# Layer 3 of a four-layer graph network interleaved with the last loop of layer 2's batch norm

## The reference, cut to what matters

```python
x = ...                                     # (128 graphs, 128 nodes, 64 features)
# layer 2: y = (adj @ h + h) @ weight + bias, rows scaled to length 1, then batch norm
cnt  = sum(mask)
mean = sum(y * m, axis=(0, 1)) / cnt
var  = sum((y - mean) ** 2 * m, axis=(0, 1)) / cnt
y    = ((y - mean) / sqrt(var + 1e-5) * gamma + beta) * m
x    = x + relu(y)
# layer 3
h = maximum(layernorm(x), 0)                # over the 64 features of each node
messages = einsum('bij,bjh->bih', adj, h)
dh = tanh(concat([h, messages]) @ W1 + b1) @ W2 + b2
x  = x + dh
```

## Time and profile before

| | us |
|---|---|
| median of 3 runs | 1461.05 |
| lowest and highest | 1458.61, 1461.1 |
| the profiled execution, its own time | 1463.7 |
| its span, first to last instruction | 1462.0 |
| final loop and row scales, 1327.5 to 1376.3 | 48.8 |
| layer 3, 1376.3 to the end | 85.7 |

### The profile page before, as it was taken

How to read it: one execution, slowest core, us unless ns; L and a number is a source line. 1 busy time by engine, 2 the same in 40 slices (tenths; PEclk the granted TensorE clock), 3 DMA queues, 4 the chain that set the end, 5 groups by cost and what they waited for, 6 DMA issues and landing times. The chain is left out here.

```text
span 1462.0 us, 41154 instructions
## 1 busy us (share of the span) xinstructions
PE 1316.5 (90%) x11243; PEld 1076.8 (74%) x11244; DVE 1154.9 (79%) x2874; ACT 1105.1 (76%) x2426; POOL 502.5 (34%) x611
## 2 busy tenths in 40 slices
PE   3999999999999999999999999997999997972398
PEld 1777777877777777777777777875889887910298
DVE  7898988899888988889888998883444445978755
ACT  4788888888888888888888888863555555916676
POOL 1343344444443344444433444431222111066400
PEclk9999999999999999999999999997999998986599
DMA  7000000000000000000000000000000000000022
GB/s 154 22 10 9 8 7 14 7 7 7 7 14 7 7 7 14 7 7 7 7 14 7 7 7 7 0 2 1 0 0 0 0 0 0 0 1 0 4 54 57
DMA packets 40925, 18.11 MB, mean 12 GB/s; under 512 B 19572, under 2 KB 40886, under 8 KB 40886
## 3 DMA queue, kind: packets, MB, share of 16 engines
q1 hardware_dynamic: 40354, 17.42, 4.8%
q10 hardware_dynamic: 532, 0.21, 0.1%
HBM read 13.44 MB, written 4.19 MB: 12 GB/s over the span
## 5 line engine op out<-in xcount | busy, mean ns | idle before, releaser
L723 DVE SCALAR_TENSOR_TENSOR acc<-slot_banks,acc 128x768 f32<-128x768 f32 x512 | 487.7, 953 | 79.5 <-PE slot_banks L442 70.6
L792 POOL TENSOR_TENSOR acc<-acc 128x384 f32<-128x384 f32 x128 | 128.1, 1001 | 529.1 <-DVE onediff L717 420.3
L442 PE MATMUL slot_banks<-ac_hi,work 128*128 128x192 f16 x1408 | 265.3, 247 | 27.3 <-DVE work L705 26.1
L442 PE MATMUL slot_banks<-ac_lo,work 128*128 128x192 f16 x1408 | 264.1, 246 | 0.0
L442 PEld LDWEIGHTS slot_banks<-ac_hi,work 128*128 (+1 forms) x1408 | 137.4, 98 | 98.4 <-issue 76.1
L442 PE MATMUL slot_banks<-ac_hi,onediff 128*128 128x192 f16 x1024 | 183.1, 246 | 6.4 <-DVE acc L723 5.1
L442 PE MATMUL slot_banks<-ac_lo,onediff 128*128 128x192 f16 x1024 | 182.3, 246 | 0.0
L442 PEld LDWEIGHTS slot_banks<-ac_lo,work 128*128 (+1 forms) x1408 | 138.2, 98 | 20.2 <-issue 14.5
L778 POOL TENSOR_TENSOR ac_lo<-ac,ac_hi 128x384 f16<-128x384 f32 x128 | 123.1, 961 | 49.3 <-ACT ac_hi L582 49.3
L542 ACT ACTIVATE work<-bank 128x512 f16<-128x512 f32 x256 | 130.7, 601 | 1.2 <-PE bank L353 1.2
L705 DVE TENSOR_SCALAR work<-work,slot_key 128x1024 f16 x256 | 117.9, 480 | 12.2 <-issue 3.7
(11 more groups left out here) (261 smaller groups left out, 3291.4 us busy)
## 6 DMA issues: line engine op xcount, KB each, us to landing
adj_in<-in_adj_dram SPq DMA_DIRECT2D x32, 256.0 KB, 2.8
out_dram<-acc SPq DMA_DIRECT2D x32, 128.0 KB, 2.0
l1w<-in_L_gnn_W_dram SPq DMA_DIRECT2D x2, 64.0 KB
l1b<-in_L_gnn_b_dram SPq DMA_DIRECT2D x2, 64.0 KB
x_all<-in_x_dram SPq DMA_DIRECT2D x4, 0.2 KB, 11.8
nm_in<-in_nodemask_dram ACTq DMA_DIRECT2D x1, 64.0 KB
w1a<-in_L_gnn_W_dram ACTq DMA_DIRECT2D x1, 48.0 KB
w1b<-in_L_gnn_W_dram ACTq DMA_DIRECT2D x1, 48.0 KB
```

Source lines behind the costliest of these rows:

```text
L442: last = nc.tensor.matmul(unit(pair, t, 1), hot(t), part[:, q, H:2 * H].unsqueeze(1), start=False, stop=(e == 1 and (t % SB == SB - 1 or t ...
L723: nc.vector.scalar_tensor_tensor(out=sums, in0=unit((q + k) % 2, 0, SU), scalar=0.0, in1=sums, op0=ALU.min, op1=ALU.add).then_inc(s_free[k ...
L792: nc.gpsimd.tensor_tensor(acc[:, q, 0:2 * H], acc[:, q, 0:2 * H], acc[:, q, 2 * H:4 * H], ALU.add)
```

## The change

The blocks of the batch norm and of layer 3 become one. `fold_in` writes VectorE's order from the final loop to the end, `fold_in_act` ScalarE's, with all chunks and pairs written out (no hardware loop). TensorE's instructions of layer 3 are the same in the same order, moved into this block; so is SyncE's loop of stores.

- Chunks of the final loop run `LEAD` = 6 ahead of layer 3's pairs: beside pair i ScalarE does the masked ReLUs of chunk i + 6 in two halves, one behind each tanh, and VectorE adds chunk i + 5 to x, takes its statistics, and scales and shifts chunk i + 7.
- VectorE does beta's addition and the addition to x for all 16 chunks (before: none and 8); GpSimd does none.
- The layer norm's scales are made for 32 graphs (4 chunks) at a time. `variances` does six VectorE operations on 32 columns; GpSimd raises the variance to the power -0.5 (`inverse_roots`, one instruction of 32 columns for each of the four parts); `scales` does one Newton step and the shift in four VectorE operations. The square root on ScalarE and the reciprocal go.
- The tanh table is loaded once ahead of the masked ReLUs; the change of blocks goes.

The core of the diff (lines before that stood in the loops and are shown above are left out):

```diff
-        s_xn = [sem(f"x_updated_layer2_{k}") for k in range(2)]
+        s_xn = sem("x_updated_layer2")
-        AHEAD = 3
+        minus_half = sb("minus_half", [N, 4 * GX])
+        LEAD = 6
+        QC = 4
+        QG = QC * GX
...
+        def scale_and_shift(dve, c):
+            v = nc.vector
+            v.tensor_tensor(g3(yc(c)), g3(yc(c)), per_feature(stat[:, 5, :]), ALU.mult).then_inc(s_ya, 1)
+            dve.wait_ge(s_ya, c + 1)
+            v.tensor_tensor(g3(yc(c)), g3(yc(c)), per_feature(beta[:, :]), ALU.add).then_inc(s_yb, 1)
+        def add_to_x(dve, c):
+            v = nc.vector
+            dve.wait_ge(s_yc, 2 * c + 2)
+            v.tensor_tensor(xc(c), xc(c), yc(c), ALU.add).then_inc(s_xn, 1)
+            dve.wait_ge(s_xn, c + 1)
+            for e in range(GX):
+                last = stats(c * GX + e)
+            last.then_inc(s_bn2, 1)
+            if c % QC == QC - 1:
+                variances(dve, c // QC)
+        def variances(dve, k):
...
+            dve.wait_ge(s_bn2, QC * k + QC)
+            v.tensor_tensor(msum[:, cols], m0, m1, ALU.add)
+            v.tensor_tensor(var[:, cols], q0, q1, ALU.add)
+            v.tensor_tensor(dif[:, cols], m0, m1, ALU.subtract).then_inc(s_lnq, 1)
+            dve.wait_ge(s_lnq, 6 * k + 1)
+            v.tensor_scalar(var[:, cols], var[:, cols], 1.0 / F, EPS, ALU.mult, ALU.add)
+            v.scalar_tensor_tensor(out=dif[:, cols], in0=dif[:, cols], scalar=0.25, in1=dif[:, cols],
+                                   op0=ALU.mult, op1=ALU.mult).then_inc(s_lnq, 1)
+            dve.wait_ge(s_lnq, 6 * k + 2)
+            v.tensor_tensor(var[:, cols], var[:, cols], dif[:, cols], ALU.add).then_inc(s_lnq, 1)
+        def scales(dve, k):
...
+            dve.wait_ge(s_root, k + 1)
+            v.scalar_tensor_tensor(out=error, in0=root, scalar=-0.5, in1=root, op0=ALU.mult, op1=ALU.mult)             .then_inc(s_lnq, 1)
+            dve.wait_ge(s_lnq, 6 * k + 4)
+            v.tensor_tensor(error, error, var[:, cols], ALU.mult).then_inc(s_lnq, 1)
+            dve.wait_ge(s_lnq, 6 * k + 5)
+            v.scalar_tensor_tensor(out=rstd[:, cols], in0=error, scalar=1.5, in1=root, op0=ALU.add, op1=ALU.mult)             .then_inc(s_lnq, 1)
+            dve.wait_ge(s_lnq, 6 * k + 6)
+            v.scalar_tensor_tensor(out=nmr[:, cols], in0=msum[:, cols], scalar=-0.5, in1=rstd[:, cols],
+                                   op0=ALU.mult, op1=ALU.mult).then_inc(s_ln3, 1)
+        def inverse_roots(pool):
+            g.memset(minus_half[:, :], -0.5).then_inc(s_minus, 1)
+            pool.wait_ge(s_minus, 1)
+            for k in range(NXC // QC):
+                cols = slice(k * QG, (k + 1) * QG)
+                pool.wait_ge(s_lnq, 6 * k + 3)
+                g.tensor_tensor(std[:, cols], var[:, cols], minus_half[:, :], ALU.pow).then_inc(s_root, 1)
+        def fold_in(dve):
...
+            for c in range(3):
+                scale_and_shift(dve, c)
+            for c in range(LEAD - 1):
+                add_to_x(dve, c)
+                if c + 3 <= LEAD:
+                    scale_and_shift(dve, c + 3)
+                if c == QC - 1:
+                    scales(dve, 0)
+            copy_sums(0, 0)
+            for i in range(NI):
+                copy_sums(i, 1)
+                if i > 0:
+                    update(i - 1, 1)
+                if i + LEAD - 1 < NXC:
+                    add_to_x(dve, i + LEAD - 1)
+                if i + 1 < NI:
+                    copy_sums(i + 1, 0)
+                update(i, 0)
+                if i + LEAD - 1 < NXC and (i + LEAD - 1) % QC == QC - 1:
+                    scales(dve, (i + LEAD - 1) // QC)
+                if i + LEAD + 1 < NXC:
+                    scale_and_shift(dve, i + LEAD + 1)
+            update(NI - 1, 1)
+        def fold_in_act(act):
...
+            nc.scalar.activation(cnt_col[:, 0:1], eps_col[:, 0:1], ACT.Tanh)
+            for c in range(LEAD - 1):
+                masked_relu(c, 0)
+                masked_relu(c, 1)
+            norm_group(0, 0)
+            norm_group(0, 1)
+            masked_relu(LEAD - 1, 0)
+            masked_relu(LEAD - 1, 1)
+            for i in range(NI):
+                for u in range(2):
+                    if i + 1 < NI:
+                        act.wait_ge(s_agg3[u], i + 1)
+                        norm_group(i + 1, u)
+                    act.wait_ge(s_lin3[u], i + 1)
+                    nc.scalar.activation(hid[:, u, 0:2 * N], bank[4 * u + 1][:, 0:2 * N], ACT.Tanh,
+                                         bias=l3b1[:, 0:1]).then_inc(s_tanh[u], 1)
+                    if i + LEAD < NXC:
+                        masked_relu(i + LEAD, u)
```

## The result

The changed kernel takes 1471.09 us (median of 6 runs, 1469.73 to 1471.84), the kernel before 1461.07 beside it. The ratio is 1.0056, with a 95% interval of 1.004 to 1.0072: 0.6% slower, where 0.94% faster was forecast (the two medians alone stand 10.0 us, 0.7%, apart).

The account below looks back on a forecast made before the run. VectorE was taken to bound the merged part; first scaling at 1327.54, plus 93.9 to pair 11 and 26.8 for the rest, gave 1448.2 us of span, corrected to 1447.3 us; range 1443 to 1457.

Parts of the forecast that it names:

- rival 1: Slow GpSimd power in the layer norm's scales: 1.0 to 2.9 us guessed; chance 0.13 for 1.5 to 4.9, 0.08 for more.
- The formula for VectorE's own wait: Over the four parts' scales, a GpSimd power of p us loses 4p - 5.7 us; 4.9 eats the whole gain.
- gap of some 6 us at a first call: At GpSimd's first power: a freshly loaded routine costs some 6 us unseen, 4.7 us once on the time, giving 1452.
- VectorE per pair, 6.00 us: Merged part: VectorE needs 3.06 us for a chunk and 2.94 for a layer 3 pair, together 6.00.
- Lead-in: Before pair 0: seven scalings with shifts, five additions with statistics and one part's scales on VectorE, together 19.8 us.
- Row scales, 1.85 us a part: Layer norm scales of 32 graphs: ten VectorE operations of 32 columns with waits, 1.85 us for each of four parts.
- Part 3, 0.5 us: At pair 11, the wait for the last part's scales, only just made, costs 0.5 us.
- Additions on GpSimd: In the final loop, 8 additions to x leave GpSimd, priced at 1.54 us each like the shifts.
- Handovers, 0.1 us a pair: Merged pairs: VectorE waits 0.1 us a pair for other engines, 1.1 us over 11 pairs.
- Rival 2: Merged pairs: handovers between in-order engines stall 0.5 us a pair, 4.4 us more, time 1451.7; chance 0.13.
- rival 3: Merged part: TensorE's clock stays low, pairs take 9.7 us instead of 6.3, time 1481; chance 0.05.
- Rival 4: VectorE's waits cost nothing: 30 scalings and additions at 0.60 instead of 0.72 us, time 1443.7; chance 0.06.

Follow-up runs that it names:

- TensorE kept busy: The changed kernel with 12 additional matmuls ahead of the neighbour sums of pairs 0, 4, 8 and 12, output unread: 1467.39 us, ratio 1.002.
- the three tails: Times from first scaling to span end, for the changed kernel with multiplications only, power on half the columns, and full power: 122.7, 132.2 and 140.3 us.
- the kernel without the power: The changed kernel with GpSimd multiplying by 0.0001 instead of raising to the power -0.5: 1450.72 us, ratio 0.9905 to the kernel before.
- the kernel with the square root: The changed kernel with ScalarE's square root and VectorE's reciprocal in place of power and Newton step: 1449.09 us, ratio 0.9903 to the kernel before.
- half a power: The changed kernel with the power on 16 of each part's 32 columns, a multiplication by 0.0001 on the others: ratio 0.9991 to the kernel before.
- The two kernels that win: The changed kernel with chunks 8 ahead and later scales, power kept: 1451.88 us; and with the square root back on ScalarE instead: 1449.09 us.
- the run of widths: The kernel before with unread powers of 8 to 128 columns and multiplications on idle GpSimd beside layer 3: 1465.38 us, beside 1464.29.

## Why the prediction was wrong

**The step that failed** is the price of the power, in rival 1. The prediction bounded it by rows of additions and selections (0.1 to 0.29 us) times a guess of ten passes, 1.0 to 2.9 us, and took the low end "since 32 columns are nearer to 0.1". It is 5.43 us, twenty times a multiplication of that width. The upper bound was no bound: no row of the trace showed any operation of that kind, and the factor of ten, like the many passes themselves, had no row behind it. With the price unknown, the slower side should have had far more than 0.08, and the range should have reached there.

**What the wait costs** was the second, smaller miss. The formula for VectorE's own wait held twice (7.1 for 7.2, 16.3 for 16.5). The prediction then let the wait stand for the whole loss. With TensorE kept busy that is what it cost: a tail of 137.1 for 120.7 + 16.5. Without, TensorE came back at the lower clock, 3.2 us more. By the three tails the point of no gain lies near 3.9 us, not at 4.9. The gap of some 6 us at a first call, for which the prediction names the Trainium skill (GPSIMD Engine Reference, Instruction dispatch), does not show either: the first power starts at 1343.75, 0.35 us after the start of the 0.19 us operation whose result it reads.

**The sum,** point by point, in the tail of 120.7 us:
- *VectorE per pair, 6.00 us:* measured 5.98 where nothing is waited for, and 6.04 on average over the six distances without a part's scales from pair 1 to pair 9 in the kernel without the power. A scaling with its shift 1.33 (1.32), an addition with statistics 1.74 (1.74). Right.
- *Lead-in:* in the kernel without the power chunk 5 is added 24.96 us after the first scaling; 24.8 by the sum. Right.
- *Row scales, 1.85 us a part:* on VectorE 0.92 us from the first variance operation to the next scaling, and 0.8 for `scales`; a part widens the distance of two additions from 5.98 to 7.82, by 1.84. Right.
- *Part 3, 0.5 us:* some 2.5 us in the kernel without the power, where TensorE's clock fell behind a wait of 2.06. The last copy starts 115.2 us after the first scaling there, 113.3 by the sum; that is the whole difference between 122.7 and 120.7. Where the clock stayed up, in the kernel with the square root, the tail is 120.9.
- *Additions on GpSimd:* the prediction priced the 8 additions that leave it at the shifts' 1.54 us; they take 1.60. Nothing hangs on it.
- *Handovers, 0.1 us a pair:* the addition of chunk 15 comes 88.05 us after the first scaling in the kernel without the power, 87.2 without and 88.3 with handovers by the sum. Right. Rival 2 did not come. The slack of ScalarE holds even two table loads a part.
- *TensorE's clock,* rival 3: 1.00 between the waits; it fell only around waits of TensorE. As an effect of rival 1 it was real, as a rival by itself it was not.
- *Rival 4,* waits for nothing: a scaling costs 0.72 us with its wait behind it and a shift 0.61. The rule of the Trainium skill (VectorE: DVE Perf Modes, The DRAIN you can't avoid) that a semaphore costs nothing extra does not hold in this trace, before or after.

**Where the gain comes from** was also told wrong: "the end of its disturbance and of its waits". Taking GpSimd out costs 3.5 us by itself in the loop as it was. The gain of 11.8 us of tail without the power must come from the merging: VectorE's work of both stages back to back, 6 us a pair, instead of a stage at 95% and one at 57% of its time, which more than pays for that part. The change of blocks, the root, the reciprocal and the table load went off the path with it (5.1 us from the end of the statistics to the first normalisation before, 1371.2 to 1376.3, row scales included, where the four parts' scales now take 7.4 of VectorE); no run separates their share from that of the overlap.

What stays open: whether the interleaving would gain more with GpSimd still shifting a share of the chunks was not tried, and no run gives the wait of half a power with the clock kept up. The two kernels that win keep TensorE's clock at 1.00 behind pair 0, up to 1440 us and beyond part 3, with waits of TensorE for a part's scales or for a copy of at most 1.7 us.

## What to carry to other kernels

An operation that has no row in the trace has no upper price: give the side on which it decides a chance that says so, or measure it by itself first, in a place where its engine is idle. In engines that work in order, a wait on the bounding one costs its length, and more where TensorE idles behind it and returns at a lower clock. And a slow operation needs either another engine or more work between its issue and its use: with the same 5.4 us power, two chunks more of lead, with the scales made one pair later, turned 0.6% slower into 0.9% faster.

## What the runs showed of the hardware

GpSimd's power in float32 takes 0.16 to 0.2 us a column over 128 partitions: 1.64 us for 8 columns, 3.07 for 16, 5.43 for 32, 10.6 for 64, 20.8 for 128; a multiplication takes 0.26 for 32 and 0.47 for 128. The first call took 5.78 in the changed kernel and 5.48 in the run of widths, so it costs 0.35 and 0.05 us more than the next. In the kernel without the power TensorE's clock fell to the lower level around a wait of 2.06 us: the first ten instructions behind it ran at the higher level, the next ones, from 1425.65 on, at the lower, until about 1429.5; in the kernel with the square root it stayed at 1.00 across a wait of 1.69 us at the same place. VectorE and GpSimd together, at 0.95 to 1.75 us for what VectorE alone does in 0.68, still do a chunk 0.2 us faster than VectorE alone.
